# Contexts of the attention in ten groups of one quad per head in place of six groups

## The reference, cut to what matters

```python
scores = jnp.einsum('bhsd,bhtd->bhst', q, k)
scores = jnp.where(mask, -jnp.inf, scores)
attn = jax.nn.softmax(scores / sqrt(D), axis=-1)
out = jnp.einsum('bhst,bhtd->bhsd', attn, v)
```

## Time and profile before

| | |
|---|---|
| median of 3 runs | 2043.42 us |
| profiled execution | 2041.5 us |
| its span | 2039.8 us |
| attention 0, heads 2 to 13 | 564.8 to 928.3 us |
| attention 1, heads 2 to 13 | 1375.6 to 1741.8 us |
| PE busy over the span | 1564.7 us (77%) |
| DVE busy | 1237.7 us (61%) |
| ACT busy | 875.0 us (43%) |

### The profile page before, as it was taken

How to read it: one execution, slowest core, us unless ns; L and a number is a source line. 1 busy time by engine, 2 the same in 40 slices (tenths; PEclk the granted TensorE clock), 3 DMA queues, 4 the chain that set the end, 5 groups by cost and what they waited for, 6 DMA issues and landing times.

```text
span 2039.8 us, 27036 instructions
## 1 busy us (share of the span) xinstructions
PE 1564.7 (77%) x8103; PEld 671.6 (33%) x8104; DVE 1237.7 (61%) x2336; ACT 875.0 (43%) x1663; POOL 411.2 (20%) x267
## 2 busy tenths in 40 slices
PE   4817756636999999999524912799999999868999
PEld 2302222321333333332213802233333333235665
DVE  2479999476777777774240115777777777324444
ACT  2353323010766667666301301166666666631111
POOL 4019989110000011010123061001001110000000
PEclk9958889965999999998757956599999999968999
DMA  2002213013111111110141122211111110000000
GB/s 69 6 29 81 82 62 114 0 51 91 36 37 48 34 37 47 36 35 13 52 132 49 50 49 93 49 37 36 48 36 35 47 45 26 13 16 8 23 15 29
DMA packets 59071, 91.76 MB, mean 45 GB/s; under 512 B 13001, under 2 KB 39057, under 8 KB 58993
## 3 DMA queue, kind: packets, MB, share of 16 engines
q1 hardware_dynamic: 56962, 86.79, 14.7%
q0 software_dynamic: 2048, 4.20, 0.9%
HBM read 74.63 MB, written 16.32 MB: 45 GB/s over the span
## 4 chain that ended last, share of the span: by engine, by line
PE 59%; DVE 23%; issue 6%; ACT 5%; POOL 3%; DMA 2%; DVEq 1%; SPq 1%; POOLq 0%; ACTq 0%
PE psum_a L870 16%; PE psum_b L840 11%; PE psum_a L852 9%; DVE arena L516 5%; DVE extra L1038 5%; DVE arena L490 3%; PE psum_a L1509 3%; PE psum_b L1509 3%; PE psum_b L326 2%; DVE extra L1041 2%; PE psum_a L326 2%; PE psum_b L1518 2%; ACT psum_a L432 2%; PE psum_a L1518 1%; POOL expert_inputs L1259 1%
## 5 line engine op out<-in xcount | busy, mean ns | idle before, releaser
L980 ACT ACTIVATE arena<-psum_a 128x512 f32<-128x512 f32 (+3 forms) x1280 | 585.6, 546 | 254.5 <-PE psum_a L852 152.5
L1038 DVE CUSTOM_DVE_ANT_0 extra<-psum_b,mask_q 128x128 bf16<-128x128 f32 (+7 forms) x512 | 365.4, 755 | 200.5 <-PE psum_b L840 200.2
L840 PE MATMUL psum_b<-arena 72*128 72x512 bf16 (+3 forms) x1280 | 362.3, 372 | 94.1 <-DMA arena<-k_parts 50.8
L852 PE MATMUL psum_a<-arena 75*128 75x512 bf16 (+3 forms) x1280 | 395.2, 357 | 11.4 <-ACT arena L980 4.5
L1041 DVE TENSOR_REDUCE extra<-psum_b 128x1 f32<-128x1024 f32 x256 | 300.6, 1219 | 64.0 <-PE psum_b L840 62.6
L870 PE MATMUL psum_a<-arena,extra 128*32 128x512 f32 x2560 | 336.6, 637 | 2.2 <-ACT arena L980 2.2
L852 PEld LDWEIGHTS psum_a<-arena 75*128 75x128 bf16 x1280 | 118.3, 98 | 337.9 <-ACT arena L980 156.7
L295 POOL TENSOR_TENSOR arena<-arena,extra 128x1024 f32<-128x1024 f32 x48 | 170.9, 3574 | 130.0 <-DVE arena L516 118.0
L840 PEld LDWEIGHTS psum_b<-arena 72*128 72x128 bf16 x1280 | 102.0, 100 | 241.4 <-DVE extra L1038 108.1
L786 POOL TENSOR_TENSOR arena<-arena 128x512 f32<-128x512 f32 x64 | 81.1, 1268 | 465.1 <-ACT arena L971 310.5
L971 ACT ACTIVATE arena<-psum_a 128x512 f32<-128x512 f32 x128 | 76.4, 597 | 137.5 <-PE psum_a L870 137.5
(11 more groups left out here) (263 smaller groups left out, 1707.8 us busy)
## 6 DMA issues: line engine op xcount, KB each, us to landing
arena<-q_parts SPq DMA_DIRECT2D x192, 96.0 KB
arena<-k_parts SPq DMA_DIRECT2D x192, 96.0 KB
extra<-c_rows SPq DMA_DIRECT2D x32, 512.0 KB, 3.6
arena<-in_L_ffn_fc_w_dram SPq DMA_DIRECT2D x32, 256.0 KB, 5.9
k_parts<-arena SPq DMA_DIRECT2D x10, 512.0 KB, 5.6
q_parts<-arena SPq DMA_DIRECT2D x6, 512.0 KB, 5.0
arena<-in_L_ffn_w_dram SPq DMA_DIRECT2D x24, 128.0 KB, 2.1
expert_inputs<-zeros SPq DMA_DIRECT2D x4, 512.0 KB, 6.0
```

Source lines behind the costliest of these rows:

```text
L840: m = e.matmul(ps[:, at:at + width], s.mq[0:ROWS, b, i * P:(i + 1) * P], s.mk[0:ROWS, b, c * CW:c * CW + width], start=True, stop=True)
L852: m = e.matmul(score_bank(p)[:, at:at + width], s.ek[0:ROWS + 3, b, j * P:(j + 1) * P], s.eq[0:ROWS + 3, b, (c + 1) * CW - width:(c + 1) * ...
L980: m = e.activation(probabilities(s, b, kind, quad, k, width), score_bank(p)[:, at:at + width], ACT.Exp)
L1038: m = e.tensor_tensor_reduce(s.unread[:, n % NB, at:at + length], ps[:, at:at + length], mask_q[:, 2 * CW - length:], 1.0, NEG, ALU.add, A ...
```

## The change

The list `SETS` gets ten groups of one quad each, chunk by chunk: diagonal quad first, then the chunk's full quads. Nothing else is edited; what is derived from the list (`NS_H`, `SET_OF`, `SET_END`, `SET_SLOT`, `CHUNK_SET`) follows.

```diff
-        SETS = [(0, [("diagonal", 0)]), (1, [("diagonal", 1), ("full", 0)]), (2, [("diagonal", 2), ("full", 1)]), (2, [("full", 2)]),
-                (3, [("diagonal", 3), ("full", 3)]), (3, [("full", 4), ("full", 5)])]
+        SETS = []
+        for c in range(NC):
+            SETS += [(c, [("diagonal", c)])] + [(c, [("full", c * (c - 1) // 2 + f)]) for f in range(c)]
         NS_H = len(SETS)
```

## The result

The changed kernel takes **1979.5 us** (median of 4 runs, 1977.2 to 1980.5) where the kernel before took 2043.1 on the same chip: a ratio of 0.9687, 95% interval 0.9670 to 0.9703, 64 us less. The forecast was 1980. The profiled execution took 1980.47, its span is 1978.7 us against 2039.8.

The account below looks back on a forecast made before the run. PE was taken as the bound, stalling because shallow buffers feed DVE and ACT. Gains of 41 + 6 + 7.6 + 8 = 63 us give 1978.5 profiled, plus 1.9 for the median: 1980 us, range 1962 to 2014, chance 0.70.

Parts of the forecast that it names:

- heads 2 to 13, stalls less switches: Twelve pairs of heads over both attentions: removed PE stalls less switch costs give 3.45 us a pair, 41 us.
- clock in these heads: PE's clock falls to 1.2 GHz in heads 2 to 13 cost 15.7 us; half, 8 us, counted as gained.
- heads 0 and 1: First heads of both attentions, taken to be like an odd head: 4 x 1.5 = 6 us gained.
- heads 14 and 15: Last heads: about 2.3 us from ACT's shorter idle in head 15, 1.5 in head 14; both attentions 7.6 us.
- the rest of the program: Other copies, signals, buffer releases and loads: no separate gain or loss entered in the sum.
- The price of a switch: On PE, each split costs 0.14 us plus 0.09 or 0.10 ahead of the burst; four splits, 0.96 us a head.
- The row of maxima: Diagonal 3 at slot 23, before `maxrow` and m2, fills PE's waits of 0.90 + 0.19; the whole 1.09 us goes.
- The other stalls of the odd head: Six other PE stalls, 1.37 us, all go because each meets a ready counterpart; the odd head gains 1.5 us net.
- The even head: Stalls of 3.5 us, including ring pieces `sum` and `turn`; 0.6 left after `turn`, 0.96 for switches, gain 1.95 us.
- Rival A: PE's stalls move and half of them stay, as DVE's pieces are uneven; 21 us gained, about 2022 us; chance 0.14.
- Rival B: Diagonal groups 1, 2 and 3 wait for ACT's copy, 2.5 us a head with switches; 2075 us, slower; chance 0.07.

Follow-up runs that it names:

- one exponential later: The changed kernel with ACT's copy of chunks 0, 1 and 2 one exponential later in its queue; ratio 0.9875 to the kernel before, median 2008.9 us.
- the run with the wait and one fall: Kernel before with diagonal 1, diagonal 2 and full 4 split off, diagonal 3 and full 3 kept as one group; ratio 0.9807, median 1999.0 us.
- the run with 1.03 us at diagonal 3 and none: The changed kernel with ACT's copies two exponentials later in its queue; ratio 1.0103 to the kernel before, median 2061.1 us.

## Why the prediction was right, and where not

The time was right to a us, but with luck: the terms erred both ways. The gain of the span was 61.1 and not 63, and this was offset by the 1.9 us that I had added for the median, which was not there: the profiled execution is 1.0 us above its median and not below it. Span times, in us:

| term | predicted | measured |
|---|---|---|
| heads 2 to 13, stalls less switches | 41 | 30.2 |
| clock in these heads | 8 | 15.7 |
| heads 0 and 1 | 6 | 6 |
| heads 14 and 15 | 7.6 | 10.6 |
| the rest of the program | 0 | -1.5 |
| sum | 63 | 61.1 |

Six pairs are 341.9 and were 357 without falls, 2 x 15.1 = 30.2; 363.5 + 366.2 - 2 x 357 = 15.7 are the falls, of which none is left.

**The price of a switch** was right: 1.00 us for a single group and 0.09 or 0.10 ahead of it, everywhere in the trace. The run with ten groups at the old slots shows that the change between the two kinds of matmul costs, and not the grouping. The rule of the Trainium skill (TensorEngine Tiling (Array Packing), Key Properties), that a change of the tiling mode drains TensorE, fits this; no run here separates the tiles from fp32.

**The row of maxima** was right, and is the firmest part: 0.96 has become 0.06, and that split alone gives half of the gain. In heads 2 to 13 half of what it gives is the clock (15.7 of 30.9 us), which the three other splits without it give back as well but for one fall.

**The other stalls of the odd head** were mis-sized. I had each of the six meet a ready counterpart; the one before m4 did not, it grew from 0.26 to 0.38, with 0.10 one piece earlier. DVE's timeline shows the step that I left out:

```profile
839.58 0.22 DVE L1053 COPY extra<-psum_b 48x128 bf16<-48x128 bf16 x1 [0.27 <-PE psum_b L845]
840.17 0.29 DVE L1039 CUSTOM_DVE_ANT_0 extra<-psum_b,mask_q 128x128 bf16<-128x128 f32 x1 [0.38 <-DVE extra L1053]
```

Between m1 and m2 DVE copies the transposed row (0.22) and then waits for its own copy to land before it frees the ring (0.38 idle). Before, this was hidden in PE's long wait. With it, DVE frees m2 0.4 us later than I had counted, about what PE waits before m4. No run takes this step away, so it is read from the trace and not tested. An odd head gained 1.2 us, not 1.5.

**The even head** keeps 0.86 after the turn where I had left 0.6, and the same 0.48 at m3 and m4. It gained 59.5 - 57.0 - 1.2 = 1.3 us, not 1.95. Rival A was partly right: of 2.5 and 3.5 us of stalls a fifth and somewhat over a third stay, not a half.

**Rival B** was rightly refused but for a reason that is too weak. ACT waits at the end of a single group, as the earlier trace rows show, but the room is a few tenths: one exponential later costs over 1%, two take more than the whole gain.

**The clock** was counted at half and gave all. The direction was right; that the falls follow the large wait alone was too simple, as the run with the wait and one fall shows, and so does the run with 1.03 us at diagonal 3 and none. On the Trainium skill's rule that I set beside it (TensorE: Matmul & The Clock Gate, on psum-queue depth-cycling: short idle gaps between groups of matmuls): these runs agree that falls can come behind a wait as short as 0.9 us, but waits of 0.86 and 1.03 us elsewhere brought none, and the ten groups of the change had no fall in these heads, so more and smaller groups did no harm there.

**The last heads** gave more than counted, 6.8 and 3.8 us in the two attentions (928.3 to 987.6 has become 905.2 to 957.7, and 1741.8 to 1798.1 has become 1683.5 to 1736.0). Head 14 was 33.8 and 30.7 us at a granted clock of 0.85 and 1.00, and is 30.7 in both at 0.94: 3.1 and 0 us, where I had counted 1.5 each. Head 15 was 25.4 and 25.7 us at 0.95 and 0.93, and is 21.8 in both at 1.00: 3.6 and 3.9 us for my 2.3. ACT's idle time behind a group there is now 0.33 and 0.26, as I had taken it. So the clock has a part in both, which I had put at nothing outside heads 2 to 13; how large it is, no run separates.

## What to carry to other kernels

In this kernel one engine feeds two others through buffers two or three deep, and the length of its own bursts mattered: a burst of 1.86 us left both without work, and they held it up right after. Where a trace shows the same, cutting the bursts can be worth while although each cut has a price on the bounding engine (here 0.24 us); put the pieces where that engine already waits, and read the wait from the distances between starts. Before moving an accumulation's first matmul forward, see where the copy that empties its bank stands in the other queue, and what stands ahead of it.

## What the runs showed of the hardware

The granted clock of PE fell from 2.4 to 1.2 GHz, in the steady heads for 3.4 us and at a cost of 1.6 us each time, behind a wait of 0.9 us in an otherwise dense stream; the same wait in 24 heads had 1, 6, 6 or 10 falls, depending on the kernel. But a wait of 1.03 us one group earlier in each of 24 heads had none, so the length of a wait alone does not tell whether the clock falls. And a move of an instruction by one place in a queue cost up to 0.38 us a head where its own length was 0.5 and its margin looked like 0.4 (ACT's copy): what it was moved behind had a wait of its own, 0.62 us.
